# Two destinations in one count cell, and more tiles counted, in the segment sums of a graph network

## The reference

```python
def sage_conv(x, edge_index, W_l, b_l, W_r, n):
    agg = segment_sum(x[src], dst, n)          # the sums that this change is about
    return agg @ W_l.T + b_l + x @ W_r.T
h   = relu(sage_conv(x, ..., 32 -> 64))
out = sage_conv(h, ..., 64 -> 32)
x   = layernorm(x + out)
x   = layernorm(x + gat(x, edge_attr, src, dst, ...))   # attention layer, not touched here
```

## Time and profile before

| | us |
|---|---|
| median of 3 runs | 4038.03 (4037.29 to 4042.26) |
| span of the profiled execution, its own time | 4039.9 |
| set-up, to the first gather | 75 |
| first sum pass | 75 to 1026 |
| node stage | 1026 to 1075 |
| second sum pass | 1075 to 1767 |
| attention stages | 1767 to 4039.9 |

### The profile page before, as it was taken

The page is one execution under the profiler, slowest core; times in us unless marked ns, Lnnn a source line. Parts: engine busy times, 40 slices in busy tenths (PEclk is TensorE's granted clock), DMA queues, the critical chain, the costliest instruction groups (busy, mean ns, idle before and its releaser), DMA issues. The chain is left out here.

```text
span 4039.9 us, 77882 instructions
## 1 busy us (share of the span) xinstructions
PE 2838.7 (70%) x25297; PEld 2329.2 (58%) x25297; DVE 2627.6 (65%) x7797; ACT 2694.4 (67%) x7435; POOL 2939.3 (73%) x2929
## 2 busy tenths in 40 slices
PE   4778887888677777775576666766666666667655
PEld 2555555666466666664465655656556666556644
DVE  8978776656243333354357777777777788777876
ACT  4979887888665566541067667776767776677745
POOL 4877777777577777745777777777777777777735
PEclk9989999999898988886557777677767777777767
DMA  3556565566688888843333333433333433333311
GB/s 86 209 181 245 215 246 215 215 223 238 237 310 289 292 301 292 285 166 95 66 85 90 82 77 89 90 91 82 84 78 87 91 87 85 77 87 87 89 30 41
DMA packets 301014, 607.50 MB, mean 150 GB/s; under 512 B 121338, under 2 KB 211892, under 8 KB 292697
## 3 DMA queue, kind: packets, MB, share of 16 engines
q1 hardware_dynamic: 207232, 517.61, 36.3%
q0 software_dynamic: 88192, 82.32, 12.2%
q10 hardware_dynamic: 5185, 2.56, 0.2%
HBM read 394.37 MB, written 207.85 MB: 149 GB/s over the span
## 5 line engine op out<-in xcount | busy, mean ns | idle before, releaser
L858 POOL DMA_INDIRECT gath<-x_parts,src_idx x652 | 729.8, 1119 | 235.2 <-issue 227.4
L1987 POOL DMA_INDIRECT scratch<-fs_scratch,src_idx x728 | 720.8, 990 | 221.9 <-issue 221.0
L914 ACT ACTIVATE scratch<-sum_x_ps_c 128x600 bf16<-128x600 f32 (+7 forms) x1003 | 769.9, 826 | 158.3 <-PE sum_x_ps_c L945 137.9
L858 POOL DMA_INDIRECT gath<-y_parts,src_idx x540 | 516.8, 957 | 169.3 <-issue 164.0
L945 PE MATMUL sum_x_ps_c<-e_tab,scratch 128*128 128x300 bf16 (+7 forms) x2006 | 485.3, 325 | 139.4 <-ACT scratch L914 75.4
L2115 ACT ACTIVATE scratch<-scratch,bias,weight 128x32 f32<-128x32 f32 x1360 | 483.9, 400 | 92.1 <-DVE bias L2185 92.1
L2029 PEld LDWEIGHTS ps_e<-fdw,scratch 128*128 128x128 f32 x3136 | 503.6, 243 | 23.7
L1016 DVE TENSOR_SCALAR e_tab<-scratch 128x1300 bf16<-128x1300 f16 (+13 forms) x1024 | 450.4, 451 | 73.9 <-PE sum_x_ps_c L945 54.7
L2029 PE MATMUL ps_e<-fdw,scratch 128*128 128x66 f32 x3136 | 486.4, 323 | 0.0
L2196 DVE SCALAR_TENSOR_TENSOR scratch<-ps_e,attn_sb 128x128 f32<-128x128 f32 x784 | 189.5, 284 | 418.2 <-PE ps_e L2029 417.3
L2095 ACT ACTIVATE scratch<-iota,dst_rel 128x128 f32<-128x128 f32 x824 | 251.2, 388 | 280.0 <-PE ps_m L2049 270.8
(11 more groups left out here) (354 smaller groups left out, 6913.9 us busy)
## 6 DMA issues: line engine op xcount, KB each, us to landing
count_scratch<-scratch SPq DMA_DIRECT2D x58, 3200.0 KB
scratch<-count_scratch SPq DMA_DIRECT2D x232, 800.0 KB
onehot<-rel_scratch SPq DMA_DIRECT2D x196, 256.0 KB
scratch<-in_edge_attr_2x SPq DMA_DIRECT2D x390, 128.0 KB
fdw<-fd_scratch SPq DMA_DIRECT2D x392, 33.0 KB
scratch<-fs_scratch,src_idx POOLq DMA_INDIRECT x728
gath<-x_parts,src_idx POOLq DMA_INDIRECT x652
gath<-y_parts,src_idx POOLq DMA_INDIRECT x540
```

The source lines that it names most:

```text
L858: pool.indirect_dma_start(out=rows_in(s, t), out_offset=None, in_=table_dram, in_offset=bass.IndirectOffsetOnAxis(ap=src_idx[:, g, k:k + 1 ...
L914: act.activation(to, ps_c[u % pairs][:, :, 0:q].rearrange("p h (d a) -> p h a d", d=d), ACT.Copy).then_inc(kept, 1)
L1987: pool.indirect_dma_start(out=rows_of(m)[:, t, :], out_offset=None, in_=fs_dram, in_offset=bass.IndirectOffsetOnAxis(ap=src_idx[:, g, k:k ...
```

## The change

Two neighbouring destinations share one count cell. An edge to the even destination adds 1 to it, one to the odd destination adds 65536. A block's cells are copied to SBUF as int32, and the same bytes are read as pairs of fp16 numbers: the low half holds the count of the one, the high half the count of the other, each as a tiny fp16 value (count x 2^-24). The products use these fp16 halves as the stationary operand, and `places` holds 2^24 in place of 1.

So a tile's cells have `span / 2 * 100` columns and not `span * 100`, and a piece of a bank holds twice the span. The classes are other ones (nine, all even, up to span 18): 1032 tiles are counted in the first pass (912 before), 1152 in all (1024 before). Only the first 48 of the first pass's blocks are stored (58 before), so the second pass counts all others. Lows are made for four tiles at a time and lie in `onehot`. The transposes of the first pass come every 20 units and not every 32. Set-up also makes each edge's weight (1 or 65536) and the halved offset.

```diff
-CLASSES = ((2, 64, 64), (3, 84, 42), (4, 64, 32), (5, 72, 24), (6, 63, 21), (7, 72, 18), (8, 80, 16), (9, 84, 14),
-           (10, 96, 12), (11, 66, 11), (12, 50, 10), (13, 99, 9), (14, 18, 9), (14, 48, 8), (15, 64, 8))
-FIRST_TILES = 912
+CLASSES = ((2, 64, 64), (4, 160, 32), (6, 160, 20), (8, 144, 16), (10, 156, 12), (12, 120, 10), (14, 180, 9),
+           (16, 112, 8), (18, 56, 7))
+FIRST_TILES = 1032
+STORED = 48
+PAIR = 65536.0
+UNPAIR = float(1 << 24)
...
-    return next(n for n in (1, 2, 4) if span * ALL_HIGHS // n <= BANK)
+    return next(n for n in (1, 2, 4) if span // 2 * ALL_HIGHS // n <= BANK)
...
-                for pieces in (2, 4):
+                for pieces in (2,):
...
+                link(dve.tensor_scalar(odd[:, 0:T1], offset[:, 0:T1], 1, None, ALU.bitwise_and))
+                link(dve.tensor_scalar(head_weight[:, 0:T1], odd[:, 0:T1], PAIR - 1.0, 1.0, ALU.mult, ALU.add))
+                link(dve.tensor_scalar(half[:, 0:T1], offset[:, 0:T1], 1, None, ALU.logical_shift_right))
...
-        TURN, APART = 150, 32
+        TURN, APART = 150, 20
...
-                counts = scratch[:, 0:COUNTS].bitcast(BF16).rearrange("p (w a q) -> p w a q", w=2, a=NK)
+                counts = scratch[:, 0:COUNTS].bitcast(F16).rearrange("p (w a q) -> p w a q", w=2, a=NK)
+                in_pairs = scratch[:, 0:COUNTS].bitcast(I32).rearrange("p (w a q) -> p w a q", w=2, a=NK)
...
-                    for b in range(len(plan.blocks) if store else 0):
+                    for b in range(STORED if store else 0):
...
-                            act.wait_ge(stored[w], b // 2 * 16)
+                            if b - 2 < STORED:
+                                act.wait_ge(stored[w], b // 2 * 16)
...
-                            to = counts[:, w, :, unit["column"]:unit["column"] + 2 * d]\
+                            to = in_pairs[:, w, :, unit["column"]:unit["column"] + 2 * d]\
...
+                    def make_lows(group):
+                        before = (group - RING + 1) * LOWS - 1
+                        if before >= plan.first_tile:
+                            dve.wait_ge(counted, counted_to(before))
+                        tiles = slice(group * LOWS, (group + 1) * LOWS)
+                        dve.tensor_tensor(lows[:, group % RING, :, :], wide(count_up[:, 0:P], 1, [P, LOWS, P]),
+                                          wide(head_low[:, tiles], 2, [P, LOWS, P]), ALU.is_equal)
...
                             d = dve.tensor_scalar(cells[:, n % RING, i * width:(i + 1) * width], count_up[:, 0:width],
-                                                  head_key[:, tile:tile + 1], None, ALU.is_equal)
-                        if both == 2:
-                            d = dve.tensor_tensor(lows[:, n % RING, :, :], wide(count_up[:, 0:P], 1, [P, 2, P]),
-                                                  wide(head_low[:, first:first + 2], 2, [P, 2, P]), ALU.is_equal)
-                        else:
-                            d = dve.tensor_scalar(lows[:, n % RING, 0, :], count_up[:, 0:P],
-                                                  head_low[:, first:first + 1], None, ALU.is_equal)
+                                                  head_key[:, tile:tile + 1], head_weight[:, tile:tile + 1],
+                                                  ALU.is_equal, ALU.mult)
...
-                                              head_rel[0:columns, b:b + 1], None, ALU.is_equal)
+                                              head_rel[0:columns, b:b + 1], UNPAIR, ALU.is_equal, ALU.mult)
...
-        segment_sum_pass("sum_y", ys_dram, flat_rest, Plan(head, head.first_blocks, HB), False)
+        segment_sum_pass("sum_y", ys_dram, flat_rest, Plan(head, STORED, HB), False)
```

More of the change, by code:

```diff
@@ L62 @@
 LEAD = 2
+LOWS = 4
 QUARTERS = 4
@@ L90, in __init__ @@
     def __init__(self):
-        self.blocks, self.units, self.items = [], [], []
+        self.blocks, self.units, self.items, self.item_of = [], [], [], []
         tile = 0
@@ L94, in __init__ @@
             pieces = pieces_of(span)
-            size = span * ALL_HIGHS // pieces
+            pairs = span // 2
+            size = pairs * ALL_HIGHS // pieces
             for _ in range(tiles // per_block):
@@ L101, in __init__ @@
                     item = len(self.items)
+                    self.item_of += [item] * step
                     banks = [(item, i, (i * pieces + piece) * size) for i in range(step) for piece in range(pieces)]
-                    self.items.append({"tiles": list(range(t, t + step)), "span": span, "first": len(self.units),
+                    self.items.append({"tiles": list(range(t, t + step)), "pairs": pairs, "first": len(self.units),
                                        "last": len(self.units) + len(banks) // 2 - 1})
                     for u in range(len(banks) // 2):
-                        self.units.append({"banks": banks[2 * u:2 * u + 2], "block": block, "span": span,
-                                           "column": (t - tile) * span, "size": size, "pieces": pieces,
+                        self.units.append({"banks": banks[2 * u:2 * u + 2], "block": block, "pairs": pairs,
+                                           "column": (t - tile) * pairs, "size": size, "pieces": pieces,
                                            "highs": slice(2 * u * ALL_HIGHS // pieces, (2 * u + 2) * ALL_HIGHS // pieces)})
@@ L122, in __init__ @@
         self.first_item = head.units[self.first_unit]["banks"][0][0]
+        self.first_tile = head.blocks[read]["tile"]
         self.end_unit = head.blocks[blocks - 1]["end"]
@@ L869, in _ @@
                     if store:
-                        sp.wait_ge(stored[0], (len(plan.blocks) + 1) // 2 * 16)
+                        sp.wait_ge(stored[0], (STORED + 1) // 2 * 16)
                     for b in range(read):
@@ L897, in keep @@
                         unit = head.units[plan.first_unit + u]
-                        b, q, d = unit["block"], unit["size"], unit["span"]
+                        b, q, d = unit["block"], unit["size"], unit["pairs"]
                         w = plan.buffer(b)
@@ L944, in count @@
                             for h, (item, i, at) in enumerate(unit["banks"]):
-                                m = pe.matmul(ps_c[u % pairs][:, h, 0:q], lows[:, item % RING, i, :],
+                                tile = head.items[item]["tiles"][i]
+                                m = pe.matmul(ps_c[u % pairs][:, h, 0:q], lows[:, tile // LOWS % RING, tile % LOWS, :],
                                               cells[:, item % RING, at:at + q], start=True, stop=True)
```

66 lines of the change are left out of this document (42 added, 24 removed).

## The result

The changed kernel takes 4005.8 us (median of 4, 4003.7 to 4010.0) against 4039.1 us before (median of 4, 4037.3 to 4042.3): a ratio of 0.9916, 95% interval 0.9902 to 0.993. It is faster by 33 us, 0.8%. Forecast were 186 us, and 4006 lies above the range of 3785 to 3950.

A forecast was written before the change was run, and what follows sets the result against it. POOL's gathers were taken to pace both passes. From 4039.9 us, 185 (first pass), 4 (second pass) and 2 (set-up) were subtracted: 3849, or 3853 with 6 us for unnamed hand-overs; range 3785 to 3950.

The forecast's parts named there:

- both passes are paced by POOL's gathers: Before the change, POOL gathers without a gap, 1.37 us each in the first pass and 1.26 in the second.
- a floor far below: First pass: PE or stores need 537 us beside the later 433 gathers, hidden by POOL with 56 us to spare.
- POOL's term: First pass: 161 us for spans 2, 4, 6, then 433 gathers at 1.37 us, 593 us.
- VectorE's term: First pass: cells 263, lows 154, one-hots 76, table adds 36, block ends 55 us; second pointer scalar free; sum 584.
- The full price of the rival: Rival: second pointer slows cell instructions to one element per cycle, first pass 980 us, total 4070 and up; chance 0.06.
- ACT's and PE's terms: First pass: ACT's int32 copies at the even price, 501 us; PE with fp16 weights at the bf16 price, 629 us.
- The stores: First pass: 8.9 us a block; 34 blocks in spans 8 to 12 held to about that, hidden behind POOL.
- a sum of stretches with one bound each: First pass: 161 us set by DVE, 593 by POOL's gathers, 12 for last block and hand-overs: 766 against 951.
- gathers get their pace back: Rival: with fewer fast VectorE instructions, first-pass gathers speed up to 1.34 or 1.26 us; total 3785 to 3835; chance 0.18.
- ACT's hand-over at 15.3 us a recounted block: Second pass: copies and products alternate on one buffer, 15.3 us per span-14 block; pass 685 to 690 us against 692.
- second pass slower: Rival: one-hots delay copies PE awaits, PE's clock drops, +60 us; total 3895 to 3950; chance 0.20, shared with DVE at half price.
- the signs that the prediction named for being wrong: Cell instructions stretch; DVE or stores leave POOL waiting over 50 us in the first pass; second pass moves over 50 us.

The follow-up runs named there:

- the kernel with three things out: Changed kernel without weight in the cell instructions, with two of 48 blocks stored and one tile gathered per slot after the first four: first pass 114 us shorter.
- thin cells: Changed kernel with first-pass cell instructions, after the first four items of each class, writing 2 columns instead of 200 to 1000: mean gather 1095 ns.
- ACT's relief: Changed kernel with the second pass's one-hots made by VectorE instead of ACT: second pass 716.5 us against 721.8.

## Why the prediction was wrong, point by point

*The step that failed first: "both passes are paced by POOL's gathers"*, with 1.37 us as a constant of the kernel and 537 us (698 with spans 2 to 6) as a floor far below. Both halves fell. A gather isn't a constant: it took 1.60 us from one to the next in the changed pass, since it lasts 946 ns where VectorE is idle at its start, and 1255 to 1677 beside cells, lows or a one-hot. And without most gathers the pass still took 830 us.

*POOL's term.* 161 + 593 = 754 us were forecast for the gathers and 854 measured: 662 busy, 157 between two, 35 waiting for PE. The prediction had looked at the share of VectorE's fast instructions, 60% falling to 46. That share did fall (by the same count, 562 of 951 to 411 of 872 us, 59 to 47%), and yet a gather grew: from 1119 to 1244 ns over the whole pass. By the prediction's own sum the share of all of VectorE's work had to rise, 584/766 = 0.76 against 0.71, and this wasn't looked at; nor that the new lows hold a gather up.

*VectorE's term, 584 us with nothing for the second pointer.* The bound was named, and the low end taken, from rows 8 whose instruction had two operations but no two pointers. Measured were 656 us. Nearly all of the difference is in the cells. Counting of each instruction only the time before the next one starts, they took 338 us in place of 263, and 281 without a weight: 56 us for the second pointer, the rest because fewer of them overlap than assumed. The lows came out as forecast (156 against 154 by the same count). To this come 53 us of waiting behind register loads. The full price of the rival (1.05 ns per element) is refuted: the price is fixed.

The Trainium skill's sentence on the second operation in the fastest mode ("VectorE: DVE Perf Modes", Mode 4×_2P) holds for the operation: 387 against 385 ns. For a pointer as its scalar I had stretched it.

*ACT's and PE's terms* were near. Copies in whole words took 714 and 1121 ns against 672 and 1007, 520 us against 501. Weight loads of fp16 took 101 to 102 ns, those of bf16 before 99 to 100. PE was busy 691 us, not 629; 652 in the kernel with three things out, at a clock of 0.99 in place of 0.94.

*The stores* did matter, 21 us (14 to 21 by the profiles of the same first pass): with two of them ACT's 31 us of waits go and VectorE's at its register loads fall from 53 to 12.

*Put together as a sum of stretches with one bound each.* That was the wrong form. Where the gathers (854) and what the others need without them (830) lie within 3% of each other, each single cure gives what its neighbours allow: 42, 38, 21, and 114 together. That this is near the 106 us by which the pass was missed (872 against 766 by the stage windows) proves nothing: the three edits also take away work that the forecast had counted.

*The rival "gathers get their pace back"* went the other way in the first pass. In the second POOL's gathers were 974 ns against 957. The Trainium skill's rule ("SBUF — State Buffer", Who interferes with whom) that a fast VectorE instruction shuts GpSimd out of the shared port speaks for longer gathers with more such work; thin cells (1249 to 1095 ns) agree. Removing the lows shortened them as well (1104 ns); these are tensor-tensor instructions, for which the page knows no two-port mode and only a claim on the read side. Gathers that found one of them under way ended 0.82 us after it, so the two-port rule covers a part of what is seen, and here the smaller one.

*Second pass, -4 us, measured +38.* The forecast's cause, ACT's hand-over at 15.3 us a recounted block, was not the bound: the block took 17.2 us (721.8/42), and ACT's relief gave 5, which is within the scatter. The failed step is that block ends were priced at 90 x 0.4 us of PE and 0.75 of VectorE, without asking for whom PE stands there: with VectorE's one-hots, moving these ends alone took the pass from 716.5 to 657.2. The rival "second pass slower" had the right sign, but its cause, the one-hots, was worth little by itself. The loads' 8.9 us a block was right as time of the DMA engines (8.8 to 9.5 in the second passes), but no pass came below 10.1 us for each block loaded.

*Right*: 532 and 412 gathers, POOL waiting in the second pass and hardly in the first, the price of the copies and products, the sign. Of the signs that the prediction named for being wrong, one came: the cell instructions got longer.

## What to carry to other kernels

Before the gain of the busiest queue is booked, take its work away in a run of its own: here POOL waited 35 us in all, and yet without most of its work only 38 of 868 us went. When a queue's pace is taken as a constant, set single entries beside what the other engines do at their start: a mean hides that a gather is 946 ns where VectorE is idle and 1677 beside a one-hot. When a producer is shortened, add the waits behind it in each consumer's order; a cure that gives nothing (ACT's one-hots, some 187 us by the estimate, gave 5) points to a wait that has taken its place, and its line in the next view of the waits says which. Price a per-partition pointer by itself, not by the operation that it feeds.

## What the hardware showed beyond that

An indirect gather on GpSimd took 946 ns where VectorE was idle at its start (152 gathers). One that found a tensor-tensor instruction of VectorE under way (512 elements in 682 ns, or 1024 in 1220) ended 0.82 us after that instruction (medians of 128 and 63 gathers).

A second pointer scalar costs a 16-bit tensor-scalar instruction a fixed 53 ns (440 against 387 at 600 elements), and 46 to 64 ns over the shapes of 200 to 700 elements; an instruction of 2 columns with both pointers takes 317 ns.

Loading window starts from memory on the chip into VectorE's registers held VectorE 53 us in 17 waits (up to 6.9 us) beside stores, and with two of 48 stores this:

```profile
DVE table_a L1112 <- issue: 11.7, 13, 1.8
```
